# Attention stage: the row products of a head group dealt to its six blocks as 6, 9, 8, 7, 8 and 4

## What is computed

```
q, k, v = h @ Wq.T + bq, h @ Wk.T + bk, h @ Wv.T + bv      # 32 heads of 32
scores = einsum('bhqd,bhkd->bhqk', q, k) / sqrt(32)
att = softmax(where(causal, scores, -inf), axis=-1)
out = einsum('bhqk,bhkd->bhqd', att, v)
x = x + ga * (out @ Wo.T + bo)
```

## Time and profile before

| what | us |
|---|---|
| median of 3 runs (lowest, highest) | 2953.43 (2952.34, 2957.43) |
| the profiled execution | 2951.61 |
| its span, first to last instruction | 2949.9 |
| PE busy | 2768.5 (94%) |
| DVE busy | 1590.3 (54%) |
| POOL busy | 1279.1 (43%) |
| ACT busy | 1052.3 (36%) |
| mean granted TensorE clock | 0.981 |

### The profile page before, as it was taken

The page is one execution under the profiler, slowest core; times in us unless marked ns, Lnnn a source line. Parts: engine busy times, 40 slices in busy tenths (PEclk is TensorE's granted clock), DMA queues, the critical chain, the costliest instruction groups (busy, mean ns, idle before and its releaser), DMA issues. The chain is left out here.

```text
span 2949.9 us, 41697 instructions
## 1 busy us (share of the span) xinstructions
PE 2768.5 (94%) x16180; PEld 1994.8 (68%) x16180; DVE 1590.3 (54%) x3165; ACT 1052.3 (36%) x1446; POOL 1279.1 (43%) x672
## 2 busy tenths in 40 slices
PE   4999999999999999799999999999999958999997
PEld 2888888888888888555555555555555527888886
DVE  4232223222313122287777777777777726777775
ACT  1322221231222111255555555555555531212121
POOL 2322332242225111267777777777777741212110
PEclk8999999999999999899999999999999989999998
DMA  7444343334336544445555555555555245454541
GB/s 247 169 163 163 133 182 140 114 118 168 114 136 188 196 168 169 119 112 116 117 121 119 122 121 121 119 120 120 122 121 116 70 128 149 143 157 129 171 128 58
DMA packets 153997, 404.87 MB, mean 137 GB/s; under 512 B 21820, under 2 KB 57076, under 8 KB 152776
## 3 DMA queue, kind: packets, MB, share of 16 engines
q1 hardware_dynamic: 123480, 292.05, 29.0%
q10 hardware_dynamic: 30320, 110.15, 17.5%
HBM read 270.41 MB, written 131.20 MB: 136 GB/s over the span
## 5 line engine op out<-in xcount | busy, mean ns | idle before, releaser
L1092 ACT ACTIVATE prob<-ps_s 128x1024 f32<-128x1024 f32 (+3 forms) x768 | 590.5, 809 | 422.0 <-PE ps_s L1230 346.4
L787 PE MATMUL ps_u<-h_hi,w_hi 128*128 128x512 f32 x1536 | 611.8, 398 | 2.0 <-POOL h_lo L555 2.0
L787 PE MATMUL ps_u<-h_lo,w_hi 128*128 128x512 f32 x1536 | 600.6, 391 | 0.0
L787 PE MATMUL ps_u<-h_hi,w_lo 128*128 128x512 f32 x1536 | 599.5, 390 | 0.0
L1048 POOL TENSOR_TENSOR added<-added,prob 128x2048 f32<-128x2048 f32 (+1 forms) x128 | 550.5, 4301 | 4.6
L549 POOL TENSOR_TENSOR w_lo<-w_raw,w_hi 128x1024 fp32r<-128x1024 f32 x93 | 222.6, 2393 | 473.1 <-ACT w_hi L617 473.0
L678 DVE SCALAR_TENSOR_TENSOR qk_lo<-ps_u,bias_col,qk_hi 128x512 fp32r<-128x512 f32 x128 | 96.0, 750 | 578.9 <-ACT qk_hi L593 578.9
L1134 DVE TENSOR_REDUCE part_high<-ps_r 128x1 f32<-128x512 f32 x496 | 335.3, 687 | 88.8 <-PE ps_r L1200 81.9
L1130 DVE CUSTOM_DVE_ANT_0 ps_r<-ps_r,row_mask 128x384 f32<-128x384 f32 (+1 forms) x500 | 310.0, 630 | 81.2 <-PE ps_r L1200 70.1
L1200 PE MATMUL ps_r<-k_st,q_st 96*128 96x512 f32 (+1 forms) x1008 | 323.1, 378 | 13.5 <-DMA v_sb<-v_tok 9.3
L787 PEld LDWEIGHTS ps_u<-h_lo,w_hi 128*128 128x128 f32 x1536 | 288.6, 188 | 61.8
(11 more groups left out here) (197 smaller groups left out, 3424.3 us busy)
## 6 DMA issues: line engine op xcount, KB each, us to landing
w_raw<-w_cols SPq DMA_DIRECT2D x72, 512.0 KB, 6.1
qk_split<-qk_hi SPq DMA_DIRECT2D x64, 512.0 KB, 2.6
qk_split<-qk_lo SPq DMA_DIRECT2D x64, 512.0 KB, 4.0
q_st<-qk_split ACTq DMA_DIRECT2D x60, 512.0 KB, 7.6
k_st<-qk_split ACTq DMA_DIRECT2D x60, 512.0 KB, 13.7
xn<-in_L_attn_x SPq DMA_DIRECT2D x8, 2048.0 KB, 12.8
v_tok<-v_out SPq DMA_DIRECT2D x32, 512.0 KB, 4.4
wm<-in_L_wmod SPq DMA_DIRECT2D x8, 2048.0 KB, 7.9
```

The lines of the kernel that those rows point to most:

```text
L787: last = nc.tensor.matmul(ps_u[u % 2][:], w[:, m, k], h[:, k, tok], start=k == 0 and j == 0, stop=k == KT - 1 and j == 2)
L1092: nc.scalar.activation(prob[:, buffer_of(t, k), 2 * pair:2 * pair + 2, off:], ps_s[pair][:, :, off:], ACT.Exp, scale=SCALE).then_inc(exp_d ...
```

## The change

Instead of one pattern of five places for all six blocks of a group (2, 1, 2, 1, 1), each block has its own; the counts of a block are now 6, 9, 8, 7, 8 and 4 instead of 7 each. The order of the 42 items and group 0's pattern stay. The two sums stay behind the last places of blocks 0 and 1; in the ring, the high sum now follows item 5 instead of 6, the low sum item 14 instead of 13.

```diff
-    SHARE = (2, 1, 2, 1, 1)
+    SHARES = ((2, 1, 1, 1, 1), (2, 2, 2, 2, 1), (2, 1, 2, 2, 1), (2, 1, 2, 1, 1), (2, 1, 2, 2, 1), (1, 1, 1, 1, 0))
+    PLACES = 5
     FIRST_SHARE = ((1, 1, 1, 1, 1), (0,) * 5) + ((2, 2, 2, 2, 2),) * (PAIRS - 2)
...
         todo, out = strewn(t), []
-        for n in range(PAIRS * len(SHARE)):
-            few = (SHARE if t > 0 else FIRST_SHARE[n // len(SHARE)])[n % len(SHARE)]
+        for n in range(PAIRS * PLACES):
+            few = (SHARES if t > 0 else FIRST_SHARE)[n // PLACES][n % PLACES]
             out.append(todo[:few])
             todo = todo[few:]
...
-        slots = per_slot(t) if t < NG else [[]] * (PAIRS * len(SHARE))
+        slots = per_slot(t) if t < NG else [[]] * (PAIRS * PLACES)
         for n, items in enumerate(slots):
             ring += items
-            if n in (len(SHARE) - 1, 2 * len(SHARE) - 1) and t > 0:
-                ring.append(("sum", t - 1, 1 if n < len(SHARE) else 0))
+            if n in (PLACES - 1, 2 * PLACES - 1) and t > 0:
+                ring.append(("sum", t - 1, 1 if n < PLACES else 0))
...
                 for p in range(PAIRS):
-                    turns = slots[p * len(SHARE):(p + 1) * len(SHARE)]
+                    turns = slots[p * PLACES:(p + 1) * PLACES]
```

## The result

The changed kernel takes 2919.86 us (median of 4 runs, 2918.9 to 2920.71), against 2955.43 (4 runs) for the kernel before on the same chips: 0.9883 of it, 95% interval 0.9871 to 0.9894. It is faster by 36 us, where 44 were forecast; 2919.86 lies inside 2893 to 2942. The profiled execution took 2918.9 us, its span is 2917.2, 32.7 less than before.

A forecast was written before the change was run, and what follows sets the result against it. TensorE's own order of work was taken as the bound. Six blocks summed to 34.60 us against 35.86, 1.26 less; with 0.2 of excess 1.46 a group, times 30 is 44 us, giving 2909.5, range 2893 to 2942.

The forecast's parts named there:

- block terms (0, 3 and 5): Windows of blocks 0, 3 and 5 in one group, forecast at 6.83, 5.50 and 3.72 us.
- The high sum's wait: Block 0: TensorE's wait for VectorE to reduce item 4 before the high sum, 0.87 us, goes whole.
- the walk of block 1: Block 1: tracing VectorE's maxima and the ring's banks, which gave new waits at products 9 and 13, 0.46 us with restarts.
- Block 1: Nine items: 0.48 us of waits for ScalarE covered, 0.51 of extra items, 0.46 of new waits; 6.60 to 7.09.
- Block 2: The extra 384-column product (0.18 us) lies inside the wait for ScalarE's load issue and costs nothing; stays 5.89.
- Block 4: A pair in place of a 512-column product, +0.05 us, giving 5.57; the turn one place earlier, not late.
- Block 5: Loses a 512-column product and a pair (0.51 us) and the shift wait (0.20): 4.43 to 3.72.
- The excess of the mean over the typical group: Mean period 0.26 us longer than the studied group's, mostly from late shift transfers; 0.2 a group given back.
- Rival A: VectorE can't keep up with nine rows in block 1: only 0.6 us a group, 18 us gained, 2935; chance 0.18.
- Rival B: No new waits in block 1, copies and banks just in time: 1.92 us a group, 58 us, 2895; chance 0.07.
- Rival C: VectorE's third low addition, held by GpSimd's first addition over SBUF reads: 3 us a group, 90 us slower, 3042; chance 0.08.
- Rival D: No effect, waits move one for one to the next late VectorE or ScalarE place: 2953; chance 0.07 with small mixtures.

The follow-up runs named there:

- e1: Kernel before with only item 6 moved behind the high sum, blocks 2 to 5 as before: 2944.54 us, 0.9966 of the kernel before.
- e2: Changed kernel with only item 6 put back ahead of the high sum: 2939.82 us, 0.9951 of the kernel before.
- e11: Against `e9`: eight items instead of nine in block 1 and nine instead of eight in block 2: 2913.44 us, 0.9865 of the kernel before.
- e8: Changed kernel with item 37 in block 5 again and the turn of the high maxima at the end of block 4: 2916.76 us.
- e9: Changed kernel with loads on SyncE, one item of blocks 2 and 3 moved ahead of the first weighing, blocks 4 and 5 as in `e8`: 2903.73 us.
- e6: Changed kernel with one item of blocks 2, 3 and 4 moved ahead of the first weighing: 2927.69 us, 0.9912 of the kernel before.
- e4: Changed kernel without GpSimd's wait for the low additions, VectorE's third low addition two items later: 3097.5 us, 1.0483 of the kernel before.

## Why the prediction was right, and where it was off

The main mechanism was right and is shown by `e1` and `e2`; three of the six block terms (0, 3 and 5) were met within 0.07 us. That the gain was missed by no more than 8 us is in part luck: the terms of blocks 2 and 4 and of the excess were too low by 16 us in all, those of blocks 0 and 1 too high by 7.

- **The high sum's wait goes in full (0.87).** Right: its load no longer waits. Block 0 is 6.84 to 6.89 us where the first score waited for the shift row, as it did in the group of the earlier trace rows, and 6.76 where it didn't; the forecast was 6.83. So about 0.84 of the 0.87 came, and what block 0 has on top goes with the shift wait. Putting item 6 back costs 20 us in the changed kernel. That it would pay alone was not claimed, and it doesn't (9 us): its follower met ScalarE's copy, an arrival that the walk of block 1 had put just in time for the changed order.
- **Block 1: covered waits 0.48, new waits 0.46.** The sum was 0.16 too high. In the group of the timeline product 9 starts 0.13 behind the mask product ahead of it, a new wait of 0.1 at most where the walk had 0.2 with the restart; product 13 starts 0.04 behind the mask product of 12, no wait where the walk had 0.26. Of the cover only one part was tested: in `e11` 0.16 came back, and the prediction had 0.17 for the second of its two waits.
- **Block 2 stays, with an extra item under the load issue.** The mis-sized term: 0 against 0.14. The cover was real, and the kernel before with its loads elsewhere puts the load issue's price at 0.40 in this block. But I walked VectorE's banks through block 1 only. Products 18 to 21 come behind a weighing with one score pair among them, and 21 waits for 18, 0.42 us at its load: VectorE had become the later one, and without the load issue the block of a typical group is not shorter.
- **Block 4: 5.57 against 5.75.** The same omission: 33 and 34, a score pair, then 35 and the turn stand behind a weighing, and product 37 behind them waits 0.15 us at its load for the maximum of 34. `e8`, whose block 4 is shorter by one pair of 0.28, is 0.38 shorter, so 0.10 of the 0.18 is this wait; the rest is not traced.
- **Block 5: 3.72 against 3.75.** Right in size: the two items are 0.51 of the 0.68, and 0.17 is left for the wait, where 0.20 was forecast. But half of its reason falls: with five items there and the turn later, blocks 4 and 5 together are even 0.08 shorter, and the waits for the shift hardly more. That no wait for the shift would be left was wrong; ten were.
- **The excess of the mean over the typical group.** I gave back 0.2 of 0.26 us, and the mean of the changed kernel is again 0.26 to 0.28 above the typical group. The means by block show why. Block 5's excess, which holds the late shift transfers, fell from 0.20 to 0.09, half of what I gave back. Block 2's rose from 0.07 to 0.12; two of its groups are over 7 us. Blocks 0 and 4 have 0.05 that they had not. With the loads on SyncE block 2 has no group over 6.4, the excess is 0.12, and 2908.46 is reached although the typical group is only 0.25 shorter (34.46); so most of block 2's part hangs on the load issue. How much comes from run to run is left open. This term (6 us) and blocks 2 and 4 (10 us), less blocks 0 and 1 (7 us), are the 9 us between the period forecast and measured.
- **Rival A** (VectorE can't keep up in block 1) did not happen in block 1, but in a milder form in blocks 2 and 4, where it wasn't looked for. **Rival B**, no new waits in block 1, came about in part: of the walk's two waits the second was not there. **Rival C** rests on a real mechanism with twice the price that I gave, but an explicit wait shuts it out, which I had missed in the code. **Rival D**, that waits move on to the next place, is what `e1` shows: 0.87 removed, 0.32 gained.

## What to carry to other kernels

In an order written by hand, a filler instruction is worth its place only: walk the helper engine (here VectorE) and its ring of banks through every block that gets more items, not only through the one where the wait was found. Here, with three banks, a fourth product between two weighings, with only one score pair among the four, waited for VectorE behind a weighing and ahead of one: 0.42 us at product 21 in the changed kernel, 0.46 at 26 in `e9`, 0.51 at 33 in `e6`. (In block 3 of `e6` it didn't, but there TensorE had just stood 0.80 us for an exponential.) Moving such a product to the other side of a weighing pays only where that side has room, and only until another engine's wait, which it had covered, comes back. And where two engines seem kept apart by timing alone, read the waits at the later one first: one line there may be the fence.

## What the hardware showed

- A VectorE addition with two operands from SBUF, 0.68 us alone, took 3.71 us when it started 1.4 us into a GpSimd addition, and ended 0.55 after that one (`e4`); the prediction had read such a pair in the earlier trace rows.
- Not expected: during the standstill of 3.2 us that this gave TensorE the granted clock fell to 0.50 and stayed there for 6.8 us, 5.9 of them with TensorE at work, which about doubled the price (178 us rather than 90).
- Not expected: 512 KB loads issued by SyncE ahead of small shift transfers in the same queue didn't delay these: three waits for them in place of ten in the changed kernel, 30 in place of 28 in the kernel before. On ScalarE's queue their issue held its exponentials by 2.3 us a group.
